# Adding D·x on GpSimd instead of by diagonal matmuls, and moving the next chunk's row exponents ahead of C·B on TensorE

## The reference, cut to what matters

```python
dA_cs = cumsum(dt * A, within a chunk)
Lmat  = exp(dA_cs[i] - dA_cs[j])
att   = where(i >= j, (C[i] . B[j]) * Lmat * dt[j], 0)        # 128 x 128 for each of 12 heads
y_intra = att @ x                                             # inside the chunk
y_inter = exp(dA_cs[i]) * (C[i] . state carried from the chunks before)
y = y_intra + y_inter + D[head] * x
y = layernorm(y) * norm_w + norm_b ;  y = y * z ;  out = y @ out_proj_w.T
```

## Time and profile before

| | |
|---|---|
| median of 3 runs | 3640.47 us (3628.37 to 3646.38) |
| the profiled execution, its own time | 3614.94 us |
| its span, first to last instruction | 3613.2 us |
| busy: TensorE, VectorE, ScalarE, GpSimd | 87%, 74%, 51%, 42% of the span |
| mean granted TensorE clock | 0.929 of full speed |

### The profile page before, as it was taken

The page is one execution under the profiler, slowest core; times in us unless marked ns, Lnnn a source line. Parts: engine busy times, 40 slices in busy tenths (PEclk is TensorE's granted clock), DMA queues, the critical chain, the costliest instruction groups (busy, mean ns, idle before and its releaser), DMA issues. The chain is left out here.

```text
span 3613.2 us, 60645 instructions
## 1 busy us (share of the span) xinstructions
PE 3140.8 (87%) x20256; PEld 1812.4 (50%) x20256; DVE 2674.8 (74%) x3983; ACT 1840.2 (51%) x4315; POOL 1507.1 (42%) x1107
## 2 busy tenths in 40 slices
PE   4888889898899998889898898998899999888965
PEld 2655547364463735547364453735446364554710
DVE  1347877778677777878778787777868778787787
ACT  1536464554636446364553646446464554646432
POOL 1014444444444344444444444344434444444455
PEclk8999999998989989999998999999989998999976
DMA  2032141413214142141412314141231413214121
GB/s 58 14 103 64 39 137 36 132 68 93 85 45 123 56 123 71 38 134 38 131 68 85 91 44 131 50 131 68 70 101 45 117 68 105 79 47 133 36 99 65
DMA packets 104163, 290.96 MB, mean 81 GB/s; under 512 B 25373, under 2 KB 27020, under 8 KB 103820
## 3 DMA queue, kind: packets, MB, share of 16 engines
q1 hardware_dynamic: 103820, 286.71, 26.3%
HBM read 181.84 MB, written 39.85 MB: 61 GB/s over the span
## 5 line engine op out<-in xcount | busy, mean ns | idle before, releaser
L747 POOL TENSOR_TENSOR hc<-hst,bcrep 128x512 f32<-128x512 f32 x768 | 1202.5, 1566 | 1178.4 <-DVE hst L1233 1143.3
L833 ACT ACTIVATE ssd<-bank,ncs 128x128 f32<-128x128 f32 x1536 | 438.8, 384 | 237.2 <-PE bank L1282 237.0
L1282 PE MATMUL bank<-hc,sel 128*32 128x512 f32 x1536 | 454.3, 677 | 101.4 <-POOL hc L747 101.4
L1220 DVE TENSOR_TENSOR wr<-durep,bcrep 128x512 f32<-128x512 f32 x768 | 521.1, 679 | 3.6 <-DMA bcrep<-bc_rows 3.6
L1233 DVE TENSOR_TENSOR_SCAN hst<-dec,wr 128x512 f32<-128x512 f32 x256 | 392.4, 1533 | 92.5 <-ACT carry L977 58.5
L1282 PE MATMUL bank<-ssd 128*128 128x32 f32 (+1 forms) x3296 | 447.2, 288 | 0.0
L936 ACT ACTIVATE bank<-durep,aneg 128x512 f32<-128x512 f32 x368 | 253.9, 690 | 294.1 <-DVE hst L1233 285.5
L1282 PEld LDWEIGHTS bank<-ssd 128*128 128x128 f32 x3296 | 399.5, 193 | 4.2
L1282 PE MATMUL bank<-ssd,wcv 64*32 64x512 f32 x5376 | 349.7, 600 | 0.0
L1282 PE MATMUL bank<-xna,wt0a 128*128 128x128 f32 (+3 forms) x1088 | 296.1, 374 | 34.1 <-DVE xnb L1044 34.1
L866 ACT ACTIVATE ssd<-bank,nbc,nwc 128x128 f32<-128x128 f32 x384 | 147.5, 453 | 345.8 <-PE bank L1428 345.8
(11 more groups left out here) (187 smaller groups left out, 5000.8 us busy)
## 6 DMA issues: line engine op xcount, KB each, us to landing
durep<-scratch SPq DMA_DIRECT2D x192, 512.0 KB, 3.7
bcrep<-bc_rows SPq DMA_DIRECT2D x128, 512.0 KB, 5.2
ssd<-stage SPq DMA_DIRECT2D x384, 140.4 KB, 2.9
ssd<-bcst SPq DMA_DIRECT2D x128, 74.4 KB, 2.7
xa<-in_x_dram SPq DMA_DIRECT2D x16, 512.0 KB, 4.0
scratch<-u SPq DMA_DIRECT2D x32, 256.0 KB, 2.1
scratch<-delta SPq DMA_DIRECT2D x32, 256.0 KB, 2.4
out_dram<-x1a SPq DMA_DIRECT2D x16, 512.0 KB, 4.8
```

The source lines that it names most:

```text
L747: nc.gpsimd.tensor_tensor(hc[:, i % CRING, :], hst[:, i % HRING, :], bcrep[:, g, 1, :], ALU.mult).then_inc(hc_ready.sem, 1)
L833: ins = nc.scalar.activation(att[:, c % 2, h, :], bank[ROW_BANKS[r]][:, k * Q:(k + 1) * Q], ACT.Exp, bias=ncs[:, c, h:h + 1])
L1220: nc.vector.tensor_tensor(wr[:, i % WRING, :], durep[:, j % SLOTS_DU, 1, :], bcrep[:, g, 0, :], ALU.mult).then_inc(w_made.sem, 1)
L1282: return nc.tensor.matmul(out, lhsT, rhs, start=start, stop=stop, skip_group_check=True)
```

## The change

D·x is no longer added by TensorE. GpSimd gets a new job, `plus_dx`, at stage 2 of a chunk (odd slots), between `states_by_c` and `layer_rstd`: it multiplies `xtok` by D of the head into `xd`, waits for `yint_ready`, and adds `xd` to `yint` (signal `yxd_ready`). For chunk 0, which has no carried state, the product goes straight to `yint`, and VectorE adds it to the bank instead of only copying. VectorE's y0 now waits for `yxd_ready` and not for `yint_ready`; ScalarE's copy to `xtok` also waits for it. D is loaded by one load (`dhead`) in place of twelve, and the three preparations of `diagd` on VectorE go away. On TensorE `rows(n,c,0)` is issued ahead of `b_by_c` of the chunk before.

```diff
-        dcol = sb("dcol", [P, XM])
-        diagd = sb("diagd", [P, XM, P])
+        dhead = sb("dhead", [P, NH])
+        xd = sb("xd", [P, DI])
...
-            for h in range(NH):
-                load(dcol[(h % 4) * HD:(h % 4 + 1) * HD, h // 4:h // 4 + 1], d0_d[h:h + 1].partition_broadcast(HD))
+            load(dhead[:, :], d0_d.partition_broadcast(P))
...
+            def plus_dx(n, c):
+
+                by_head = xtok[:, c % 2, 0:DI].rearrange("p (h d) -> p h d", d=HD)
+                factor = bc(dhead[:, :].unsqueeze(2), [P, NH, HD])
+                if c == 0:
+                    nc.gpsimd.tensor_tensor(yint[:, 0, :].rearrange("p (h d) -> p h d", d=HD), by_head, factor,
+                                            ALU.mult).then_inc(yxd_ready.sem, 1)
+                    return
+                pool.wait_ge(yxd_ready.sem, yxd_ready.at(n, c))
+                nc.gpsimd.tensor_tensor(xd[:, :].rearrange("p (h d) -> p h d", d=HD), by_head, factor,
+                                        ALU.mult).then_inc(xd_made.sem, 1)
+                pool.wait_ge(xd_made.sem, xd_made.at(n, c))
+                pool.wait_ge(yint_ready.sem, yint_ready.at(n, c))
+                nc.gpsimd.tensor_tensor(yint[:, c % 2, :], yint[:, c % 2, :], xd[:, :], ALU.add).then_inc(yxd_ready.sem, 1)
...
                 if c >= 0:
                     if c < NCH - 1:
                         scaled_x(n, c)
+                    else:
+                        pool.wait_ge(xt_copied.sem, xt_copied.at(n, NCH))
+                c = chunk_at(s, 2)
+                if c >= 0:
+                    plus_dx(n, c)
                 c = chunk_at(s, 4)
                 if c >= 0:
                     layer_rstd(n, c)
...
                         act.wait_ge(state_ps.sem, state_ps.at(n, c - 1))
+                        act.wait_ge(yxd_ready.sem, yxd_ready.at(n, c - 1))
                     nc.scalar.copy(xtok[:, c % 2, :], bank[B_XY][:, :]).then_inc(xt_copied.sem, 1)
...
-                if c == 0:
-                    ins = nc.vector.tensor_copy(y0[:, 0, :], bank[B_XY][:, 0:DI])
-                else:
-                    dve.wait_ge(yint_ready.sem, yint_ready.at(n, c))
-                    ins = nc.vector.tensor_tensor(y0[:, c % 2, :], yint[:, c % 2, :], bank[B_XY][:, 0:DI], ALU.add)
-                ins.then_inc(y0_ready.sem, 1)
+                dve.wait_ge(yxd_ready.sem, yxd_ready.at(n, c + 1))
+                nc.vector.tensor_tensor(y0[:, c % 2, :], yint[:, c % 2, :], bank[B_XY][:, 0:DI], ALU.add).then_inc(y0_ready.sem, 1)
...
-                for m in range(XM):
-                    mm(bank[B_XY][:, m * P:(m + 1) * P], xs[m][:, t], diagd[:, m, :], m == 0, False)
                 pe.wait_ge(att_ready.sem, att_ready.at(n, c + 1))
                 for h in range(NH):
                     ins = mm(bank[B_XY][:, h * HD:(h + 1) * HD], att[:, c % 2, h, :],
-                             xtok[:, c % 2, h * HD:(h + 1) * HD], False, h == NH - 1)
+                             xtok[:, c % 2, h * HD:(h + 1) * HD], h == 0, h == NH - 1)
...
-                c = chunk_at(s, 2)
-                if c >= 0:
-                    b_by_c(n, c)
                 c = chunk_at(s, 0)
...
                     rows(n, c, 0)
+                c = chunk_at(s, 2)
+                if c >= 0:
+                    b_by_c(n, c)
```

More of the change, by code:

```diff
@@ L354, in build @@
         yint_ready = sig("yint_ready", NCH - 1)
+        xd_made = sig("xd_made", NCH - 1)
+        yxd_ready = sig("yxd_ready", NCH)
         y_ps = sig("y_ps", NCH)
@@ L1009, in _ @@
                                                 bc(w.unsqueeze(2), taps), ALU.mult).then_inc(s_prep, 1)
-            for m in range(XM):
-                nc.vector.tensor_scalar(diagd[:, m, :], ident[:, :], dcol[:, m:m + 1], None, ALU.mult).then_inc(s_prep, 1)
             dve.wait_ge(s_wev, copies[-1] + 2)
@@ L1606 @@
 EXP_LN = "natural_log_exp_and_others"
-NLOADS = 76
-PREPS = 15
+NLOADS = 65
+PREPS = 12
 DVE_STEPS = 35
```

## The result

| | before | after |
|---|---|---|
| median of 4 runs | 3641.64 us (3628.37 to 3646.38) | 3533.43 us (3522.22 to 3536.63) |
| ratio, 95% interval | | 0.970 (0.967 to 0.973): faster |
| the profiled execution, its own time | 3614.94 us | 3522.22 us |
| its span | 3613.2 us | 3520.5 us |
| mean granted TensorE clock | 0.929 | 0.921 |

The change takes 108 us off the median. The forecast was 118 us and 3523; the time is 10 us above it and inside the range of 3490 to 3572.

A forecast was written before the change was run, and what follows sets the result against it. TensorE bounds the kernel from chunk 1 on. Per image 5.4 + 2.6 - 1.0 = 7.0 us, 113 with the first pass, 118 with the start, off 3640.5: 3523 us, range 3490 to 3572.

The forecast's parts named there:

- Diagonal matmuls, 5.4 us per image.: On TensorE between C by state and y0: removing them saves 0.67 us in all eight chunks of an image.
- Order on TensorE, 2.6 us per image.: Rows put ahead of C·B fill TensorE's 0.68 us wait for ScalarE, gaining 0.65 us in four intervals per image.
- VectorE late next.: Whether VectorE's chain becomes the bound: no, intervals of 12.59 become 11.3 us, with 0.8 us to spare on it.
- GpSimd's work in steady intervals at nothing.: Product and sum, 0.83 and 0.95 us, hide in GpSimd's 3.54 us wait for lve; room before the scan 0.3 us.
- the fourth rival: VectorE and GpSimd take turns at their shared port in each interval, adding 0.9 + 1.9 us: 3720 us, chance 0.03.
- The give-back of 1.0 us per image.: In an image's first two intervals GpSimd's new work holds up VectorE; 1.0 us lost, bounds nothing to 1.5.
- Start, 5.1 us.: Eleven fewer loads of D on SyncE's queue let TensorE begin 5.1 us sooner.
- "The tail of an image after the last chunk moves up whole.": Stretch behind an image's last chunk: it shifts earlier at unchanged length, so the chunks' gain is kept in full.
- growing tails: Sign of a wrong prediction: the tails of images grow by what the chunks lost.
- a rival of 3540: TensorE's lower clock level reaches the first interval of all images, adding 16.5 us: 3540 us, chance 0.12.
- the first rival: VectorE becomes the bound if GpSimd's product and sum each run 1.8 us or more: 3588 us, chance 0.11.
- the forecast's bound of 3555: Upper bound of the forecast: the 0.8 us spare on VectorE's chain used up and 1.5 us per image given back.

The follow-up runs named there:

- The threefold product: Changed kernel with GpSimd's product of D·x made three times for each chunk from 1 on: 3556.50 us, ratio 0.982.
- filled kernels: Unread matmuls put into TensorE's two waits for the state and two waits in the tail: kernel before 3571.18 us, changed kernel 3449.15 us.
- second trace of the changed kernel: The changed kernel, unaltered, measured once more beside later kernels on the same chip: 3538.71 us, ratio 0.978.

## Why the prediction was right, and where its sum was off

**Diagonal matmuls, 5.4 us per image.** Right. 0.67 us went from every interval, as the kernel with D·x alone shows (11.39 to 10.72, 11.25 to 10.58, 12.60 to 11.93). Seven of the eight lie between the y0 of an image, 4.69 us.

**Order on TensorE, 2.6 us per image.** Right, in mechanism and size: 2.65 us by the kernel with the order alone, and one wait of 0.68 left in each image.

**VectorE late next.** Right: the interval is 11.27 against 11.3, TensorE is busy for 11.23 of it, and VectorE waits 1.66 us in front of y0. The rival needed product and sum of 1.8 us each; they took 0.83 and 1.00, as their shortest neighbours had said.

**GpSimd's work in steady intervals at nothing.** Right, with a room of 0.26 in front of the scan where 0.3 was forecast. The threefold product shows what lies behind that edge: not 2.8 us per interval, as the fourth rival had it, but 0.8 at most; in the interval shown one state product is held up.

**The give-back of 1.0 us per image.** The mechanism was right and the size too large: 0.59 us. The prediction placed two collisions. The one of chunk 0's product with what already crowds there is real, but it stretches the input product behind the scan and costs 0.59 us ahead of the first y0. The one of chunk 1's sum with the scan doesn't happen: the sum has ended before the scan begins, and the intervals 0 to 1 and 1 to 2 are the same with and without D·x.

**Start, 5.1 us.** TensorE's first transpose comes 6.1 us sooner, the first y0 5.4.

**The sum.** By the measured terms it is 5.4 + 2.65 - 0.6 = 7.4 us per image, 119 over sixteen, and with the start 125. The first pass gave 5.2 us between its y0 in the profiled pair and 7.4 between the filled kernels. The two filled kernels differ by 122 in the medians and by 116 in the spans. So the sum of 118 was good for kernels whose waits are filled.

**"The tail of an image after the last chunk moves up whole."** This is the step that failed; the prediction had named growing tails as a sign of being wrong, and the sum had no term for the clock. In the profiled pair the tails grew by 25.9 us, a quarter of what the chunks gained, and in the second trace of the changed kernel by 15.9. TensorE's time at the lower level follows from the mean clock, as twice the missing part times the span: 2 x 0.071 x 3613 = 513 us before, 2 x 0.079 x 3520 = 556 after. With the waits filled on both sides the growth of the tails is 7 us, no more than the give-back of 0.59 in each of them explains, and the measured gain 122. By these differences the clock takes 14 us of the change in the first comparison and 31 in the second, and 23 by the spans of the profiled executions (116 - 93): 19 in the tails (25.9 - 7.1) and 8 in the chunks, whose stretches together are 11.6 us longer than filled before and 19.4 after; the ends of the kernel take 4 off that. It was named, as a rival of 3540 that would cost 16.5 us, but for another place: all images were to have a first interval of 13.04. Instead 3 of the later images have two long intervals (13.40 and 12.70) where 6 had one (the prediction had counted 5), which costs 5 us more than before (3 x 4.85 = 14.6 against 6 x 1.65 = 9.9 us), and the larger part fell in the tails.

**The number.** 3523 was forecast and 3533 measured. That it came so near is in part luck: the second measurement gave 3539, also inside the range, and in the profiled pair the gain was 93 us, 25 less than the sum. The missing 10 us have the size of the clock's part, but they are less than the 17 us by which the gain differs between the two comparisons, so they can't be split further.

**Slips in the working.** By its own terms the first rival's sum ends 14.5 us after y0 and not 14.7 (10.7 + 0.1 + 1.8 + 0.1 + 1.8), and the forecast's bound of 3555 doesn't come out of the terms given with it. Neither touches the forecast or the range.

What stays open: why the clock falls behind one wait of the tail in one image and behind another in the next, and what of that the change brings about; and why the mean clock can rise to 0.956 without a gain.

## What to carry to other kernels

Read what an edit is worth from the interval that it shortens, with the wait that ends last in it; both parts of this change showed there to a few hundredths of a microsecond, while two comparisons of the same kernels differed by 17 us in the gain. An engine that idles through a gap can take work up to about the length of that gap at next to no cost, even if it is slower at it; look for the one place where there is no gap, here the first chunk of an image, where it cost 0.59 us. When work is taken off TensorE, look at its waits elsewhere: the clock can take part of the gain back behind them, and seven unread matmuls per image in waits of 1.5 to 3 us were worth 90 us here, nearly as much as the change.

## What the runs showed of the hardware

- TensorE's granted clock fell behind single waits of 1.5 to 3 us between busy stretches, in some images and not in others. In the changed kernel a tail at a mean clock of 0.88 took 138.97 us and the next image's, at 0.91, 132.63. With unread matmuls in the waits the changed kernel went from 3538.71 to 3449.15 us.
- A higher mean clock is no gain by itself: a median of 3449.15 us went with 0.942 to 0.946, and 3447.44 with 0.952 to 0.958.
- GpSimd's product xw took 2.44 us beside VectorE (2020.90) against 0.82 at its shortest, with no effect on the interval; VectorE's scan took 2.12 us beside hc on GpSimd (1937.90) against 1.23 at 2015.55; VectorE's product of the state went from 0.54 to 1.42 in the kernel with three products, and TensorE then waited 0.58 us. A long duration costs only where the chain passes.
- On GpSimd the product of 128x384 with a factor per head took 0.83 us in the median of 112 (0.82 to 1.15) and the sum 1.00; on VectorE they took 0.75 and 0.56.
